# Mixing the experts' outputs: diagonal products on TensorE for six of eight token groups, last product on VectorE

## The reference

```
idx1, idx2 = best and second-best expert of the token
w1 = gate1 / (gate1 + gate2 + 1e-9);  w2 = gate2 / (same)
out = ye[idx1, pos1] * (w1 * keep1) + ye[idx2, pos2] * (w2 * keep2)
g = silu(out)
x = x + s * g
```

## Time and profile before

| | us |
|---|---|
| median of 3 timed runs | 1086.83 (1086.61 to 1087.13) |
| the profiled execution | 1089.36 |
| its span, first to last instruction | 1085.6 |
| busy: PE, DVE, ACT, POOL | 959.3, 685.5, 640.1, 659.2 |
| mean granted clock of TensorE | 0.968 |

### The profile page before, as it was taken

One profiled execution on the slowest core, in us unless ns is written; L12 is line 12 of the kernel. 1 busy time (PEld: TensorE's weight loads), 2 busy tenths in 40 slices (PEclk: granted clock), 3 DMA queues, 4 the chain that ended last, 5 costly groups with the idle time before them and its releaser, 6 DMA issues.

```text
span 1085.6 us, 21561 instructions
## 1 busy us (share of the span) xinstructions
PE 959.3 (88%) x6286; PEld 688.3 (63%) x6286; DVE 685.5 (63%) x2575; ACT 640.1 (59%) x1968; POOL 659.2 (61%) x811
## 2 busy tenths in 40 slices
PE   6588889999999969999998998999998999999840
PEld 2455556666659966666665665655666878999830
DVE  6857976776773326767776768677774563455316
ACT  4349657767665547677775675575764653444334
POOL 5553668788855534667765588788736632555423
PEclk9789989999999999999999999999999999999985
DMA  9200202302427762123023031230232154777765
GB/s 301 58 6 1 46 23 62 71 26 62 116 64 208 225 200 65 31 48 78 22 47 68 6 69 37 58 78 20 65 67 60 33 152 123 229 223 230 209 169 146
DMA packets 95441, 103.16 MB, mean 95 GB/s; under 512 B 10095, under 2 KB 83030, under 8 KB 95088
## 3 DMA queue, kind: packets, MB, share of 16 engines
q1 hardware_dynamic: 88752, 89.36, 31.6%
q0 software_dynamic: 6592, 12.65, 3.4%
HBM read 77.54 MB, written 23.50 MB: 93 GB/s over the span
## 4 chain that ended last, share of the span: by engine, by line
PE 57%; DVE 20%; ACT 7%; issue 6%; DMA 5%; POOL 3%; SPq 1%; POOLq 0%; DVEq 0%; ACTq 0%
PE bank L1231 11%; PE bank L1260 7%; PE bank L715 7%; PE bank L726 6%; PE bank L1287 6%; PE bank L1275 4%; PE bank L1250 4%; DVE arena L1882 4%; ACT arena L1616 3%; PE bank L1310 3%; DMA expert_out<-RA 2%; DVE arena L1891 2%; DVE arena L1786 2%; DMA expert_out<-arena 1%; PE bank L1486 1%
## 5 line engine op out<-in xcount | busy, mean ns | idle before, releaser
L1616 ACT ACTIVATE arena<-arena 128x128 f32<-128x128 f32 (+1 forms) x512 | 226.8, 446 | 110.0 <-DVE arena L1882 109.5
L1882 DVE CUSTOM_DVE_ANT_0 arena<-bank,arena 128x128 f32<-128x128 f32 (+1 forms) x512 | 183.1, 412 | 130.4 <-PE bank L1260 127.0
L1231 PE MATMUL bank<-arena 128*128 128x512 f32 x384 | 211.8, 638 | 8.4 <-ACT arena L1605 4.9
L1006 POOL TENSOR_TENSOR arena<-arena 128x512 f32<-128x512 f32 x128 | 133.4, 1045 | 140.2 <-ACT arena L1592 134.9
L1891 DVE COPY arena<-bank 128x384 f32<-128x384 f32 x256 | 130.1, 549 | 20.8 <-PE bank L1275 20.3
L1021 POOL TENSOR_TENSOR arena<-arena 128x512 f32<-128x512 f32 x128 | 129.1, 1046 | 1.3
L684 POOL DMA_INDIRECT expert_out<-arena x71 | 70.0, 986 | 96.7 <-issue 42.9
L1592 ACT ACTIVATE arena<-bank 128x512 f32<-128x512 f32 x192 | 112.6, 587 | 26.4 <-PE bank L1231 26.2
L1260 PE MATMUL bank<-arena 64*128 64x128 f32 (+1 forms) x1024 | 120.0, 353 | 9.3 <-DVE arena L1882 8.7
L1275 PEld LDWEIGHTS bank<-const,arena 128*128 128x128 f32 x768 | 91.2, 142 | 55.9 <-issue 55.5
L1287 PE MATMUL bank<-arena 128*64 128x256 f32 (+1 forms) x1024 | 112.2, 340 | 5.1 <-DVE arena L1891 4.4
(11 more groups left out here) (292 smaller groups left out, 1635.1 us busy)
## 6 DMA issues: line engine op xcount, KB each, us to landing
arena<-in_wp SPq DMA_DIRECT2D x40, 514.0 KB
arena<-recip_rows SPq DMA_DIRECT2D x30, 512.0 KB, 6.8
XN<-in_wp SPq DMA_DIRECT2D x24, 514.0 KB
arena<-expert_rows SPq DMA_DIRECT2D x46, 129.0 KB, 3.1
arena<-in_b SPq DMA_DIRECT2D x64, 64.0 KB
arena<-expert_out SPq DMA_DIRECT2D x16, 256.0 KB, 5.2
expert_out<-fill SPq DMA_DIRECT2D x11, 338.6 KB, 7.6
expert_rows<-fill SPq DMA_DIRECT2D x1, 2644.5 KB, 20.7
```

The lines of the kernel that those rows point to most:

```text
L1006: pool.tensor_tensor(sq[:, i % 2], r, r, ALU.mult).then_inc(S["sq_done"], 1)
L1231: mm = pe.matmul(RING[bnk][:, :], xa[:, p, t * P:(t + 1) * P], wqkv[:, 512 * k:512 * k + 512], start=True, stop=True)
L1616: ins = act.activation(w, w, ACT.Exp, bias=nm[:, p, 16 * t + h:16 * t + h + 1], scale=-1.0, accum_out=den[:, p, 16 * t + h:16 * t + h + 1])
L1882: ins = v.tensor_tensor_reduce(out=SPb[:, c % 2, 384 * k + P * t:384 * k + P * t + n], in0=SBANK[k][:, P * t:P * t + n], in1=alibi[:, h, N ...
```

## The change

Parts 0, 1, 3, 4, 6 and 7 (`BYPE`) are mixed on TensorE: for each tile and expert a 128x128 diagonal matrix of the gate weights is multiplied with the expert's rows, and the two products are summed in PSUM. ScalarE's Silu reads that PSUM bank. The diagonals are built by VectorE behind expert blocks 28 to 33, one part's eight behind each block, with two instructions of 128x512 (identity times weight), in arena columns that hold nothing by then. Parts 2 and 5 (`BYDVE`) are mixed as before. The product with the attention output moves from GpSimd to VectorE. The order of the parts after the loads is 0, 1, 3, 2, 4, 6, 5, 7 (`LAST`); the loads keep the order 0 to 7. A one-column Silu on ScalarE behind the last Gelu (`warm`) brings its function table's load forward.

```diff
@@ -248,6 +248,12 @@
         OF = arena[:, O1:2 * FC1 - O1].rearrange("p (k n) -> p k n", k=2)[:, :, 0:NT * D].rearrange("p k (t d) -> p k t d", d=D)
         GA = arena[:, 0:2 * NT * D].rearrange("p (k t n) -> p k t n", k=2, t=NT)
 
+        BYPE, BYDVE = (0, 1, 3, 4, 6, 7), (2, 5)
+        at[0] = FC1 + NT * D
+        DG = take(len(BYPE) * 4 * 2 * D).rearrange("p (q t k n) -> p q t k n", t=4, k=2, n=D)
+        warm = take(1)
+        LAST = (0, 1, 3, 2, 4, 6, 5, 7)
+
         def ffn_buffers(wb, b2b, xb, hT, xbT, yb, idx):
             return (wb.rearrange("p (i n) -> p i n", i=NBUF), b2b.rearrange("p (i n) -> p i n", i=NBUF),
                     xb.rearrange("p (i t n) -> p i t n", i=NBUF, t=2), hT.rearrange("p (i n) -> p i n", i=2),
@@ -292,7 +298,7 @@
...
 
         class Chain:
 
@@ -857,6 +863,8 @@
         RANK_STEP = {FB + 5: 0, FB + 7: 1, FB + 9: 2}
         RB = lambda b: bass.ds(b * N, N)
 
+        MIXB = bank[2:6] + bank[0:2] + bank[6:8]
+
         block = ctx.enter_context(nc.Block())
 
 
@@ -978,9 +986,9 @@
                 for k in range(2):
                     sp.dma_start(GA[:, k, 4 * q:4 * q + 4], yt[1][k * T:(k + 1) * T, :].rearrange("(t p) d -> p t d", p=P)[:, 4 * q:4 * q + 4])\
                       .then_inc(S[f"y1_in{q}"], 16)
-            for q in range(8):
+            for n, q in enumerate(LAST):
                 s = slice(4 * q, 4 * q + 4)
-                sp.wait_ge(S["out_ready"], q + 1)
+                sp.wait_ge(S["out_ready"], n + 1)
                 sp.dma_start(out_v[:, s], RA[:, 512 * q:512 * q + 512].rearrange("p (t d) -> p t d", d=D))\
                   .then_inc(S["out_done"], 16)
             sp.wait_ge(S["out_done"], 16 * 8)
@@ -1155,15 +1163,6 @@
             last_rows()
             pool.wait_ge(S["filled"], 16 * (1 + NFILL))
             ffn_send(pool, 1, NBLK1, NBLK0)
-
-            def product(q):
-                sl = slice(4 * q, 4 * q + 4)
-                pool.wait_ge(S["silu_done"], q + 1)
-                pool.tensor_tensor(OF[:, 1, sl], OF[:, 1, sl], GA[:, 0, sl], ALU.mult).then_inc(S["mixed_in"], 1)
-
-            pool.wait_ge(S["attn1_done"], NT // 4)
-            for q in range(8):
-                product(q)
 
 
         @block.tensor
@@ -1557,6 +1556,16 @@
             ffn_tensor(pe, 1, NBLK1, NBLK0, loads1)
 
 
+            pe.wait_ge(S["ye_evac"], NBLK0 + NBLK1)
+            for n, q in enumerate(BYPE):
+                pe.wait_ge(S["diag_ready"], n + 1)
+                pe.wait_ge(S[f"y1_in{q}"], 32)
+                for t in range(4):
+                    for k in range(2):
+                        mm = pe.matmul(MIXB[q][:, t * D:(t + 1) * D], DG[:, n, t, k], GA[:, k, 4 * q + t], start=(k == 0), stop=(k == 1))
+                mm.then_inc(S["mixed"], 1)
+
+
         @block.scalar
         def _(act):
 
@@ -1763,17 +1772,22 @@
                 ins.then_inc(S["second_scaled"], 1)
 
             def silu(q):
-                act.wait_ge(S["mixed"], q + 1)
                 g = GA[:, 0, 4 * q:4 * q + 4, :]
-                act.activation(g, g, ACT.Silu).then_inc(S["silu_done"], 1)
+                if q in BYPE:
+                    act.wait_ge(S["mixed"], BYPE.index(q) + 1)
+                    ins = act.activation(g.rearrange("p t n -> p (t n)"), MIXB[q][:, :], ACT.Silu)
+                else:
+                    act.wait_ge(S["mixed_sums"], BYDVE.index(q) + 1)
+                    ins = act.activation(g, g, ACT.Silu)
+                ins.then_inc(S["silu_done"], 1)
 
             act.wait_ge(S["gate_exp"], 2)
-            second(0)
-            second(1)
-            for q in range(8):
+            act.activation(warm, ones[:, 0:1], ACT.Silu)
+            for n, q in enumerate(LAST):
                 silu(q)
-                if q + 2 < 8:
-                    second(q + 2)
+                for m in LAST[n + 2:n + 3]:
+                    if m in BYDVE:
+                        second(m)
 
 
         @block.vector
@@ -2086,6 +2100,13 @@
                 if j == NB + NT // 4 + 3:
                     v.wait_ge(S["dve_step"], link.n)
                     v.sem_inc(S["gate_exp"], 1)
+                if j > NB + NT // 4 + 3:
+                    n = j - NB - NT // 4 - 4
+                    sl = slice(4 * BYPE[n], 4 * BYPE[n] + 4)
+                    for k, W in enumerate((G1W, G2W)):
+                        ins = v.tensor_tensor(DG[:, n, :, k], ident.unsqueeze(1).to_broadcast([P, 4, D]),
+                                              W[:, sl].unsqueeze(2).to_broadcast([P, 4, D]), ALU.mult)
+                    ins.then_inc(S["diag_ready"], 1)
 
             norm_rows(len(SETS) - 2)
             v.wait_ge(S["ring_evac"], RING_ALL)
@@ -2141,27 +2162,35 @@
             for b in range(12, NB):
                 step1(b)
             residual(NB - 1)
-            ffn_vector(v, 1, NBLK1, NBLK0, loads1, 28, behind)
+            ffn_vector(v, 1, NBLK1, NBLK0, loads1, 28 + len(BYPE), behind)
 
             def mix(q):
                 v.wait_ge(S[f"y1_in{q}"], 32)
-                v.wait_ge(S["second_scaled"], q + 1)
+                v.wait_ge(S["second_scaled"], BYDVE.index(q) + 1)
                 for i in range(4 * q, 4 * q + 4):
                     ins = v.scalar_tensor_tensor(out=GA[:, 0, i], in0=GA[:, 0, i], scalar=G1W[:, i:i + 1], in1=GA[:, 1, i],
                                                  op0=ALU.mult, op1=ALU.add)
-                ins.then_inc(S["mixed"], 1)
-
-            def combine(q):
+                ins.then_inc(S["mixed_sums"], 1)
+
+            def product(n, q):
                 sl = slice(4 * q, 4 * q + 4)
-                v.wait_ge(S["mixed_in"], q + 1)
+                v.wait_ge(S["silu_done"], n + 1)
+                v.tensor_tensor(OF[:, 1, sl], OF[:, 1, sl], GA[:, 0, sl], ALU.mult).then_inc(S["mixed_in"], 1)
+
+            def combine(n, q):
+                sl = slice(4 * q, 4 * q + 4)
+                v.wait_ge(S["mixed_in"], n + 1)
                 v.tensor_tensor(xr[:, sl], xr[:, sl], OF[:, 1, sl], ALU.add).then_inc(S["out_ready"], 1)
 
-            for q in range(8):
-                mix(q)
-                if q >= 2:
-                    combine(q - 2)
-            combine(6)
-            combine(7)
+            v.wait_ge(S["attn1_done"], NT // 4)
+            for n, q in enumerate(LAST):
+                for m in LAST[n + 1:n + 2]:
+                    if m in BYDVE:
+                        mix(m)
+                product(n, q)
+                if n:
+                    combine(n - 1, LAST[n - 1])
+            combine(7, 7)
 
 
 # ---- launch: one core; inputs and outputs as the reference has them ----
```

More of the change, by code:

```diff
@@ L294, in block_kernel @@
             *[f"y1_in{q}" for q in range(8)], "second_scaled", "first", "tables_ready", "turned1", "mixed", "silu_done", "mixed_in", "l1w_in", "l1w_ready", "z1_full", "z1_evac", "v1_full", "v1_evac", "s1_full", "ttr1_done", "exp1_done", "pt1_full",
-            "pt1_evac", "o1_full", "rd1_done", "rd_layer1", "o1_done", "attn1_done", "copied", "pads_ready", "first3", "copy_ids", "recip_half0", "recip_half1", "gate_exp", "out_ready", "out_done", "wexp")}
+            "pt1_evac", "o1_full", "rd1_done", "rd_layer1", "o1_done", "attn1_done", "copied", "pads_ready", "first3", "copy_ids", "recip_half0", "recip_half1", "gate_exp", "diag_ready", "mixed_sums", "out_ready", "out_done", "wexp")}
         class Chain:
```

## The result

The changed kernel takes 1076.73 us (median of 4 runs, 1073.19 to 1078.49); before, 1086.98 us. The ratio is 0.9887, with a 95% interval of 0.9852 to 0.9922: 10.25 us or 1.1% faster (8.5 to 16.1 us by the interval). Forecast was 1080.2 us in a range of 1078.5 to 1084.3, a gain of 6.6. The direction was right, the range missed: some four microseconds more are gone than the forecast had terms for. The forecast counted on telling 2.2 us from nothing; by the intervals, the totals of this study are known to 3 to 8 us either way, so that the four microseconds had to be found in distances within the traces.

A forecast was written before the change was run, and what follows sets the result against it. The tail was taken to be bound by VectorE's 2.68 us period, eight times, and by the loads after the change. Span 1085.6 - 6.6 = 1079.0 us; median 1086.83 should become 1080.2 us, range 1078.5 to 1084.3.

The forecast's parts named there:

- Gain: 6.6 us: Tail: the last output lands at 74.3 instead of 80.9 us (leading 10 omitted).
- 0.60 us apart: Tail on VectorE: each product and combine priced at 0.60 us, with 0.68 as upper bound.
- 1.95 us at 2.4 GHz: Tail on TensorE: a part is 16 records, 1.95 us at the full clock, 3.4 at 1.2 GHz, at most 3.8.
- Part 7 is not what is late: part 6 is, by its landing: End of tail: part 7's Silu ends at 69.1, before its product's turn at 69.7, so part 6's load landing decides.
- The diagonals hidden: Behind expert blocks 28 to 33: two VectorE products a block, 1.28 to 1.36 us, fit the waits for sends and cost nothing.
- The table load worth nothing: ScalarE's 1.28 us table load, moved ahead of the loads, gains nothing because the first Silu waits for TensorE at 56.2.
- None of this moves: Tail's sixteen loads: issued from 1048.9 us, last landed about 1066.2, unaffected by the change.
- The 4.7 us from there to the end of the span I leave as they are.: From the last output's landing at 1080.9 us to the end of the span: 4.7 us, kept unchanged.
- A tail at 1.2 GHz throughout: Rival: TensorE's clock stays low, a part costs 3.4 us, gain 2.6, time 1084.2 us; chance 0.12.
- Transfers: Rival: tail outputs pile up behind loads in SP's queue at 1.3 us each; gain 4.3, time 1082.5 us; chance 0.10.
- The slower rival: Experts' loop: diagonals and GpSimd hold each other up, exposing 7.65 us; time 1087.9 us; chance 0.05.
- the stall of 1.03 us: Tail mixing on VectorE: if GpSimd's product isn't the cause, remaining mixings take 2.15 us; 1080.8 us, inside the forecast.

The follow-up runs named there:

- b_diag: The kernel before plus the twelve VectorE products that build the diagonals, which nothing reads; ratio to the kernel before 1.0004 (0.9975 to 1.0032).
- b_dve_prod: The kernel before with all eight tail products on VectorE instead of GpSimd, mixing left on ScalarE and VectorE; ratio 0.9928 (0.9893 to 0.9962).
- a_gp_prod: The changed kernel with the tail's products back on GpSimd, mixing still as changed; ratio to the kernel before 0.9945 (0.9912 to 0.9979).

## Why the prediction was right or wrong

**The tail was right.** "Gain: 6.6 us" was made from 80.9 - 74.3, both about the last load's landing at 66.2: 14.7 us before and 8.1 after. Measured are 14.78 and 8.12. Term by term:

- Product and combine "0.60 us apart": seven in a row from 1064.02 to 1068.32, 4.3 us, as forecast. The two mixings left: 1.14 forecast, 1.14 and 1.13 measured.
- TensorE, 16 records a part and not eight, "1.95 us at 2.4 GHz": 32 in 3.81, 1.9 a part. At the lower clock 3.4 to 3.6 was said: the first 32 records took 6.23 us with the clock's return in them, and part 0's Silu began 52.84 - 49.05 = 3.8 us after TensorE. The count of records mattered: part 6's 2.04 us on TensorE stand in the chain that ends last, and with 1.07 in their place the forecast would have had the end 0.9 us too early.
- "Part 7 is not what is late: part 6 is, by its landing": the chain's last landing is part 6's, and TensorE starts on it at 1061.33.
- The last landing 2.6 us after issue: 2.6. The last two outputs of the changed kernel:

```profile
L992 SPq DMA_DIRECT2D out<-RA x2: 372/372/373, 1067.7 to 1068.3; - x2
...
DMA to landing us min/median/max: 2.3/2.5/2.6
```

- The diagonals hidden: b_diag has 1.0004, to within 3.5 us, and in the changed kernel VectorE still waits for a send behind each of the six pairs.
- The table load worth nothing: no run leaves it in its old place. For it speaks that ScalarE idles 11.14 us ahead of part 0's Silu (row at 1052.84), in which 1.28 would fit.
- The loads, of which it was said "None of this moves": the last landed 17.70 us after the first load's issue, not 17.3, and 17.16 before. The totals are too coarse to show it, and the cause is open.

**The step that failed** is one sentence: "The 4.7 us from there to the end of the span I leave as they are." The forecast put at nothing what the change does to this stretch, and gave no reason. A trace of its cause stood in the chain of before, the row at 1076.19 us (POOLq L125), on an engine that the change takes out of the tail. The row shows where the drain starts, not how long it lasts: the chain ends with the last combine and is silent on the 4.7 us behind. The runs showed two things in it: 0.4 us that an execution has after its last landing where nothing else is late, and 4.3 us in which the program waits for GpSimd's drain. Moving the products to VectorE makes GpSimd's work end 30 us sooner (from 28.9 us behind the first load's issue to 1.6 ahead of it), and the drain runs beside the loads. With that term the forecast is 1086.8 - 6.6 - 4.3 = 1075.9 us, 0.8 from the median.

The range failed by the same step: its lower end, 1.7 us below the forecast, allowed for shorter hand-overs and a sooner landing, and had no bound for the epilogue, although that was the one stretch that was carried over without a reason. The bounds that the prediction gives for its terms, 0.5 and 0.3 us, don't add up to these 1.7 us either; even so the range is missed by 1.8.

**The rivals.** The clock came back some 5 us after TensorE began: 0.81 in the window from 1053 to 1056 means 0.50 up to 1054.1. A tail at 1.2 GHz throughout isn't what ran. Transfers don't bind: the last outputs landed after 2.3 and 2.6 us, as before. The slower rival, diagonals held up by GpSimd's sends, is refuted at its price of 7.65 us by b_diag (at most 3.5) and by the pairs of 1.28 us; what is left of it is that a send gets 0.2 us longer (last section). That the stall of 1.03 us might not be GpSimd's is refuted by b_dve_prod. What the part moved to TensorE and the part moved to VectorE give each is seen in column C: products off GpSimd 2.6 us alone (14.8 to 12.2), mixing on TensorE alone 4.4 (14.8 to 10.4), both 6.7. Of the drain's 4.3 us the first alone gives all; the second alone gives 1.5 (D is 3.21 in a_gp_prod), since the last product ends further ahead of the last landing.

Left open is why the stretch ahead of the tail varies as it does (it did so in both kernels), and whether the loads really come later in the changed one. Neither was tried.

## What to carry to other kernels

Account for the distance between the last landing and the end of the span before calling it fixed: ask which engine's closing drain ends last. GpSimd's stands 7.5 us behind its last instruction here, so its work should end some 7.4 us or more before the last output lands (7.5 + 0.23 - 0.41), and one column at the end brings the same drain as 512. Where VectorE and GpSimd share two-input work over SBUF, count an overlapping pair as one after the other; VectorE doing both was faster here. And cut a tail at events whose distance the code alone decides: between landing and landing, executions of one kernel agreed within 0.1 us that differed by 20 to 30 in their spans.

## What was not expected of the hardware

The drain: 7.51 to 7.53 us behind GpSimd's last instruction in all fourteen traces, whatever that instruction was.

A send of GpSimd that runs beside VectorE's two-input products is longer, and the products are not. The timeline of the changed kernel, GpSimd beside VectorE's diagonals:

```profile
1010.55 1.28 DVE L2107 TENSOR_TENSOR arena<-const,small 128x512 f32<-128x512 f32 x2
...
1011.49 1.20 POOL L690 DMA_INDIRECT expert_out<-arena  x1 [1.47 <-DVE arena L813]
...
1012.99 0.98 POOL L690 DMA_INDIRECT expert_out<-arena  x1 [0.30 <-issue]
...
1014.22 1.28 DVE L2107 TENSOR_TENSOR arena<-const,small 128x512 f32<-128x512 f32 x2
...
1015.15 1.20 POOL L690 DMA_INDIRECT expert_out<-arena  x1 [1.19 <-DVE arena L813]
```

The sends at 1011.49 and 1015.15, which begin while diagonals are built, take 1.20 us, and the one at 1012.99 takes 0.98. Each of the six pairs of diagonals has such a send of 1.20 beside it, in b_diag too. The 1.17 us of the earlier trace rows, beside a two-input product too, fits that. Next to a product of GpSimd a two-input instruction of VectorE that comes second stands until that product is over (1375 ns in the earlier trace rows, 1734 in a_gp_prod), and a product that comes second is longer too (1.58 us at 1076.22 in the kernel before, where a combine had begun at 1076.01); next to a send VectorE loses nothing, and the send loses 0.2 us. The Trainium skill (SBUF — State Buffer, section Who interferes with whom) has the first as a lock that the loser waits out whole, and the traces agree; of the second it says only that a VectorE instruction with two SBUF inputs contends with what reads SBUF on GpSimd.
